# Attention stage of a macaron block: row maxima 1.75 steps ahead instead of 2, projections and value copies moved within the step, another order in the SyncE and GpSimd queues

## The reference, cut to what matters

```python
def _L0_attn_ref(x, wq, bq, wk, bk, wv, bv, wo, bo, gamma, beta):
    B, S, E = x.shape
    H = 16; D = E // H
    Q = x @ wq + bq; K = x @ wk + bk; V = x @ wv + bv
    Q, K, V = (a.reshape(B * H, S, D) for a in (Q, K, V))
    scores = jnp.einsum('bqd,bkd->bqk', Q, K) / jnp.sqrt(jnp.float32(D))
    attn = jax.nn.softmax(scores, axis=-1)
    ctx = jnp.einsum('bqk,bkd->bqd', attn, V).reshape(B, S, E)
    out = ctx @ wo + bo + x
    mu, var = jnp.mean(out, -1, keepdims=True), jnp.var(out, -1, keepdims=True)
    return (out - mu) * jax.lax.rsqrt(var + LN_EPS) * gamma + beta

x = x + 0.5 * ffn(layernorm(x))
x = x + attn(layernorm(x))
x = x + 0.5 * ffn(layernorm(x))
```

## Time and profile before

| What | us |
|---|---|
| profiled execution: span | 813.9 |
| profiled execution: device time | 816.08 |
| median of three runs | 816.56 |
| PE busy | 646.0 (79%) |
| DVE busy | 599.6 (74%) |
| ACT busy | 458.5 (56%) |
| POOL busy | 408.8 (50%) |
| attention steps | from about 225 to 635 of the span |

### The profile page before, as it was taken

One profiled execution on the slowest core, in us unless ns is written; L12 is line 12 of the kernel. 1 busy time (PEld: TensorE's weight loads), 2 busy tenths in 40 slices (PEclk: granted clock), 3 DMA queues, 4 the chain that ended last, 5 costly groups with the idle time before them and its releaser, 6 DMA issues.

```text
span 813.9 us, 16314 instructions
## 1 busy us (share of the span) xinstructions
PE 646.0 (79%) x5121; PEld 283.7 (35%) x5121; DVE 599.6 (74%) x1550; ACT 458.5 (56%) x1057; POOL 408.8 (50%) x559
## 2 busy tenths in 40 slices
PE   4896577632699999999999999999999776667760
PEld 3643455421222222222222232222223533445540
DVE  4788834446878989999899998999983779844430
ACT  5653222210158878888888888888888544222220
POOL 5576778854523234344343443434211448578763
PEclk9997755665579999999999999999999568755665
DMA  7898444325544454454545545455421213443334
GB/s 197 235 252 230 94 75 65 52 24 144 96 87 115 100 116 122 104 128 104 123 113 111 122 102 125 111 112 122 104 58 40 68 29 92 110 88 67 60 42 116
DMA packets 242983, 86.66 MB, mean 106 GB/s; under 512 B 169992, under 2 KB 235688, under 8 KB 242856
## 3 DMA queue, kind: packets, MB, share of 16 engines
q1 hardware_dynamic: 226048, 73.05, 37.8%
q0 software_dynamic: 12288, 10.49, 8.7%
q10 hardware_dynamic: 4584, 2.39, 1.0%
HBM read 56.23 MB, written 31.49 MB: 108 GB/s over the span
## 4 chain that ended last, share of the span: by engine, by line
PE 30%; DVE 26%; POOL 13%; issue 13%; ACT 7%; DMA 7%; SPq 1%; ACTq 0%; POOLq 0%; DVEq 0%
DVE arena L1122 14%; PE psum L1752 8%; PE psum L1743 8%; POOL sums L692 7%; ACT arena L1453 4%; DMA sums<-sums_sb,sidx 4%; POOL arena L667 4%; PE psum L1728 4%; DVE arena L1135 3%; PE psum L1533 2%; DMA arena<-dispatch_rows,arena 1%; DVE arena L1130 1%; PE psum L1692 1%; DVE arena L939 1%; PE psum L1550 1%
## 5 line engine op out<-in xcount | busy, mean ns | idle before, releaser
L1122 DVE TENSOR_REDUCE arena<-psum 128x2 f32<-128x1024 f32 x256 | 306.0, 1212 | 36.3 <-PE psum L1730 36.3
L1453 ACT ACTIVATE arena<-psum 128x512 f32<-128x512 f32 x512 | 278.3, 598 | 72.1 <-PE psum L1743 71.2
L1743 PE MATMUL psum<-arena 122*128 122x512 bf16 x512 | 164.4, 387 | 7.0 <-ACT arena L1453 3.5
L1752 PE MATMUL psum<-arena 128*32 128x512 f32 x1024 | 138.2, 610 | 0.0
L692 POOL DMA_INDIRECT sums<-sums_sb,sidx x64 | 102.0, 1594 | 41.2 <-issue 19.4
L1728 PE MATMUL psum<-arena 48*128 48x512 bf16 x256 | 88.4, 400 | 17.0 <-DMA arena<-qk_parts 7.9
L784 POOL TENSOR_TENSOR arena<-arena 128x128 f32<-128x128 f32 x30 | 14.0, 466 | 149.5 <-DVE arena L1135 149.5
L1730 PE MATMUL psum<-arena 48*128 48x512 bf16 x256 | 88.4, 401 | 0.0
L1743 PEld LDWEIGHTS psum<-arena 122*128 122x128 bf16 x512 | 42.7, 100 | 130.1 <-ACT arena L1453 123.5
L667 POOL DMA_INDIRECT arena<-dispatch_rows,arena x64 | 64.1, 1002 | 27.9 <-issue 17.9
L1610 PE MATMUL psum<-ident,arena 128*128 128x128 f32 x64 | 25.0, 413 | 54.6 <-DMA arena<-dispatch_rows,arena 54.5
(11 more groups left out here) (152 smaller groups left out, 1178.9 us busy)
## 6 DMA issues: line engine op xcount, KB each, us to landing
ctx<-arena SPq DMA_DIRECT2D x32, 256.0 KB, 2.1
arena<-qk_parts SPq DMA_DIRECT2D x127, 64.0 KB
qk_parts<-arena SPq DMA_DIRECT2D x32, 192.0 KB, 3.8
arena<-qk_parts SPq DMA_DIRECT2D x190, 32.0 KB
arena<-qk_parts SPq DMA_DIRECT2D x63, 96.0 KB
arena<-lists SPq DMA_DIRECT2D x16, 256.0 KB, 3.5
sums<-x_sb SPq DMA_DIRECT2D x16, 256.0 KB, 4.6
arena<-ctx SPq DMA_DIRECT2D x64, 64.0 KB, 2.4
```

The source lines that it names most:

```text
L1122: dve.tensor_reduce(mx_r[r % 2][:, p:p + 9:8], src, X, ALU.max).then_inc(a_mx, 1)
L1453: act.activation(p_r[tau % NPB], bank[4 + tau % 2][:, :], ACT.Exp, scale=SCALE).then_inc(a_P, 1)
L1743: pe.matmul(bank[4 + tau % 2][:, :], keys, heads(q_st[r], rows, g), start=True, stop=True)\
L1752: ins = pe.matmul(bank[6][32 * g:32 * g + 32, :], v_r[r][:, g, kt, :], p_r[(4 * kt + g) % NPB], start=(kt == 0), stop=(kt == 3), tile_posi ...
```

## The change

`HEAD = 6`: before step 0 only 6 of the 8 row maxima of tile 1 are taken. Step n takes the last two of tile n+1 (slots 0 and 1 on DVE, tau 1 on PE), then splits the maxima of tile n+1 in high and low, then takes the first six of tile n+2. PE turns the maxima of tile n+1 at tau 7 instead of 3, and ACT copies them after tau 7. `v(n+3)` goes from before slot 10 to behind the first `pv` (tau 3), its copy on DVE from slot 4 to slot 1. `qk(n+4)` goes from tau 6 to tau 10, its copy from after tau 7 to after tau 11. POOL does `center(t+1)` ahead of `split(t)`. In the SP queue `ctx_store` and `max_rows` change places, and `ctx_load` goes ahead of `stack_store`. The normalisations on ACT are put on other slots. No instruction is added or removed.

```diff
+    HEAD = 6
...
-            uses += [u for u in (("x", n + 4), ("m", n + 1), ("q", n + 4), ("v", n + 3), ("o", n - 2))
+            uses += [u for u in (("x", n + 4), ("v", n + 3), ("m", n + 1), ("q", n + 4), ("o", n - 2))
...
@@ SyncE
                     if mid or n + 3 < end:
                         stack_load(n + 3, (r + 3) % NBUF)
+                    if mid or n >= 1:
+                        ctx_store(n - 1, (r - 1) % NBUF)
                     if mid or n + 1 < end:
                         max_rows(n + 1, (r + 1) % NBUF)
                     if mid or n >= 1:
-                        ctx_store(n - 1, (r - 1) % NBUF)
+                        ctx_load(n - 1, (r - 1) % NBUF)
                     if mid or n + 4 < end:
                         stack_store(n + 4, r)
-                    if mid or n >= 1:
-                        ctx_load(n - 1, (r - 1) % NBUF)
@@ GpSimd
-                    split(t, t % NBUF)
                     if t + 1 < NT:
                         center(t + 1, (t + 1) % NBUF)
+                    split(t, t % NBUF)
@@ VectorE
-                for p in range(8):
+                for p in range(HEAD):
                     row_max(1, 1, p)
-                max_high(1, 1)
-                max_low(1, 1)
...
-                        if n + 2 < NT:
-                            row_max(n + 2, at(2), p)
+                        ahead, part = divmod(HEAD + p, 8)
+                        if n + 1 + ahead < NT:
+                            row_max(n + 1 + ahead, at(1 + ahead), part)
+                            if part == 7:
+                                max_high(n + 1 + ahead, at(1 + ahead))
+                                max_low(n + 1 + ahead, at(1 + ahead))
...
-                        if p == 4 and n + 3 < NT:
+                        if p == 1 and n + 3 < NT:
                             v_copy(n + 3, at(3))
...
-                    if n + 2 < NT:
-                        max_high(n + 2, at(2))
-                        max_low(n + 2, at(2))
@@ ScalarE
-                        if tau == 3 and n + 1 < NT:
+                        if tau == 7 and n + 1 < NT:
                             max_copy(n + 1, (r + 1) % NBUF)
...
-                        if tau == 7 and n + 4 < NT:
+                        if tau == 11 and n + 4 < NT:
                             qk_copy(n + 4, r)
-                        if tau in (11, 15) and n >= 6 and n % GT == 2:
+                        if tau in (11, 13, 14, 15) and n >= 6 and n % GT == 2:
+                            z_norm(n - 6 + (11, 13, 14, 15).index(tau))
+                        if tau in (7, 15) and n >= 8 and n % GT == 0:
                             for t in (0, 1):
-                                z_norm(n - 6 + (tau - 11) // 2 + t)
-                        if tau in (7, 11) and n >= 8 and n % GT == 0:
-                            for t in (0, 1):
-                                x_norm(n - 8 + (tau - 7) // 2 + t)
+                                x_norm(n - 8 + (tau - 7) // 4 + t)
@@ TensorE
-                        if tau == 6 and (mid or n + 4 < end):
+                        if tau == 10 and (mid or n + 4 < end):
                             qk(n + 4, r)
-                        if tau == 10 and (mid or n + 3 < end):
-                            v(n + 3, at(3))
...
-                        if tau == 3 and (mid or n + 1 < end):
+                        if tau == 7 and (mid or n + 1 < end):
                             maxT(n + 1, at(1))
                         if tau == 3 and (mid or n >= 1):
                             pv(n - 1, at(-1), 3)
+                        if tau == 3 and (mid or n + 3 < end):
+                            v(n + 3, at(3))
...
-                        if tau % 4 == 1 and (mid or n + 2 < end):
-                            scores(n + 2, at(2), tau // 2)
-                            scores(n + 2, at(2), tau // 2 + 1)
+                        if tau % 4 == 1:
+                            ahead, p = divmod(HEAD + tau // 2, 8)
+                            if mid or n + 1 + ahead < end:
+                                scores(n + 1 + ahead, at(1 + ahead), p)
+                                scores(n + 1 + ahead, at(1 + ahead), p + 1)
...
-                for p in range(8):
+                for p in range(HEAD):
                     scores(1, 1, p)
```

More of the change, by code:

```diff
@@ L1229, in attention @@
                             x_var((n - 7) // GT)
-                        if n == NT - 2 and p == 1:
+                        if n == NT - 2 and p == 2:
                             xT_copy(0)
@@ L1761, in step @@
                             xT(n + 4, r)
-                        if tau == 6 and (mid or n + 4 < end):
+                        if tau == 10 and (mid or n + 4 < end):
                             qk(n + 4, r)
-                        if tau == 10 and (mid or n + 3 < end):
-                            v(n + 3, at(3))
                         if tau == 14 and (mid or n >= 2):
                             proj(n - 2, at(-2))
-                        if not mid and n == NT - 2 and tau == 2:
+                        if not mid and n == NT - 2 and tau == 6:
                             pe.wait_ge(a_mx, 8 * NT)
                             transposes(ffns[1], 0, 0)
-                        if not mid and (n, tau) in ((NT - 2, 10), (NT - 1, 2), (NT - 1, 10)):
+                        if not mid and (n, tau) in ((NT - 2, 12), (NT - 1, 2), (NT - 1, 10)):
                             g = 2 * (n - (NT - 2)) + tau // 8
```

## The result

Four runs of the changed kernel gave 839.23 to 844.04 us, median 840.81; the kernel before took 816.95 us beside it (816.33 to 817.97). The ratio is 1.0297, with a 95% interval of 1.0272 to 1.0321: about 24 us slower. The forecast was 829.0, 12 us slower. The range of 818 to 846 holds the result, and the direction and the mechanism are right, but the forecast change is half of the one that came.

The account below looks back on a forecast made before the run. The SP queue's cycle was to bind the steps: 3.80 + 6.12 + 2.18 + 0.97 + 0.10 = 13.17 us against 12.69. Over 27 cycles step 29 begins 12.8 us later, giving 829.0 us, range 818 to 846.

Parts of the forecast that it names:

- What bounds the kernel: Engines together bound the old step of 12.69 us; in the new order the SP queue's cycle, 13.17 us, binds.
- The signs that I named: New profile: equal steps of about 13.2 us, PE waiting for L459, SP hardly for POOL, `ctx_load` near 0.93 us.
- The cycle, 13.17 us: SP queue from one `stack_store` to the next: 3.80 + 6.12 + 2.18 + 0.97 + 0.10 us.
- Rival 1: In the SP queue `ctx_load` keeps 2.12 us, so the cycle is 14.3 us and the time 860; chance 0.12.
- `stack_store` behind `ctx_load`, 0.1 us: SP queue: issuing the store after `ctx_load` adds 0.1 us a cycle, bounds 0 and 1.2.
- Beginning and end: Step 2 begins at 251.6, 1.5 us earlier; steps 29 to 31 change by 0, within 1 us.
- Engines at nothing: Moves on PE, ACT and DVE cost nothing under the wait for `max_rows`; uncovered, -15 to +8 us in 27 steps.
- The 0.28 us behind the +8: Upper bound of what the moves on PE's chain add to an engine-bound step of 12.69 us.
- Rivals 2 to 4: Cycle doesn't bind: engines gain, 800 to 802 (0.05); `v` costs, 822 (0.06); parts cancel, 816 to 818 us (0.03).
- rival 2: Shorter landings keep the SP cycle from binding and DVE's idle time is filled: 800 to 802 us; chance 0.05.

Follow-up runs that it names:

- e1: The changed kernel with the SP queue back in the old order, all other edits kept: 822.66 us, ratio 1.0106.
- e2: The kernel before with only the new order of the SP queue: 835.95 us, ratio 1.0267.
- e3: The changed kernel with `ctx_store` ahead of `stack_load` in the SP queue: 821.45 us, ratio 1.0070.
- e4: The changed kernel with `ctx_load` behind `stack_store` again in the SP queue: 823.32 us, ratio 1.0101.

## Why the prediction was right in kind and short in size

- *What bounds the kernel:* right. The two waits laid bare in the SyncE queue close a cycle longer than the step; e1 to e4 show it from four sides. The signs that I named came: the wait for the split vanished, PE waits for L459 at the first `scores_t`, `ctx_load` takes 0.93 us. The steps are not of equal length, though: cycles run from 13.16 to 14.50 us.
- *The cycle, 13.17 us:* this is the step that failed. I took each term from an undisturbed row or a median, as if all 27 cycles were undisturbed; the cycle needs the mean, 13.60. The 10 cycles without an `instruction` transfer take 13.25, so the sum was right for those, and the other 17, at 13.80, make some 9 of the 12 us that are missing. Of the miss of 0.43 us a cycle, `stack_store` to `stack_load` has 0.25 (4.15 us where I had 3.80 and 0.10), the 16 issues 0.13 (6.25 where I had 6.12), the rest 0.05. The rows for it lay in the profile of before: with its means, 3.99 and 6.28 us, the same sum is 13.5, and 27 times 0.35 puts 9 us on the forecast, about 838. Rival 1, a `ctx_load` of 2.12 us, didn't happen. The 13.60 lies in the range that I had given the cycle, 12.95 to 13.65, but at its upper end.
- *`stack_store` behind `ctx_load`, 0.1 us:* nearly right. Its median landing went from 3.8 to 4.0.
- *Beginning and end:* step 2 began at 250.5, forecast 251.6. Step 29 to the end of the span changed by 0.9 us, forecast 0 within 1.
- *Engines at nothing:* right while the queue covers them (1.0297 against 1.0267 for the order alone). For the case without that cover I had -15 to +8 us; e1 shows 7 to 9. The 0.28 us behind the +8 doesn't follow from the rows named, where 0.39 less 0.16 is 0.23, and I had let `qk` "take v's place" without pricing that it is 0.64 us where `v` was 0.39.
- *Rivals 2 to 4:* all needed a cycle that doesn't bind, and it binds. (With the estimates of 2.45 and 2.6 us the sum beside rival 2 is 12.2, not 12.1.)

## What to carry to other kernels

A queue that issues in order is an engine: sum its issues and the waits for landings that stand between them, and compare the sum with the step before reordering it. A store directly ahead of what waits for its landing turns slack into path. And once a chain has no slack, price it with means, since every late landing and stalled issue that a slack used to swallow is then paid in full. Look at where the late ones lie, too: here the first 7 of the 27 cycles average 14.06 us and the other 20 13.44, so rows from the middle of a stage alone are too kind.

## What the runs showed of the hardware that was not expected

Small irregularities of the SyncE queue are frequent: the 16 issues of `stack_load` take 6.05 to 6.1 us in most cycles, but 6.3 to 7.2 in about a third, and single issues of 0.42 us have taken 1.56. Landings of the same 192 KB store had a median of 4.0 us and a maximum of 5.2. In the changed kernel the landings above 4.1 us all coincide with a transfer of the kind `instruction`, and so do 9 of the 10 single issues of `stack_load` above 0.46 us (the tenth is the first one, ahead of the steps). And with the queue's order as before, a version with `qk` at tau 6 and the maxima 1.75 steps ahead beats both kernels, 808.16 us, ratio 0.9878.
